# Mixture-of-experts half of a transformer block: experts written out without loops, routing two blocks ahead, expert weights spread by DMA and multiplied in on GpSimd

## What is computed

```python
x = x + attention(layernorm(x))        # 32 x 256 tokens, width 128, 16 heads, window of 128
h = layernorm(x)
scores = sigmoid(h @ gate_w.T)         # 16 experts in 4 groups
# the two best groups by (scores + bias), then the four best experts in them
w = picked scores / their sum * 2.5    # 12 of the 16 weights of a token are 0
g = einsum('th,eih->eti', h, gate_proj);  u = einsum('th,eih->eti', h, up_proj)
y = sum over experts of w[t,e] * ((silu(g) * u) @ down_proj[e].T)
x = x + y + (silu(h @ sh_gate.T) * (h @ sh_up.T)) @ sh_down.T
```

## Time and profile before

| | |
|---|---|
| runs | 808.34 us median of 3 (807.64 to 811.28) |
| the profiled execution's own time | 805.08 us |
| its span, first to last instruction | 803.3 us |
| mean granted TensorE clock | 0.966 of full speed |
| PE, DVE, ACT, POOL busy | 745.7, 599.4, 370.6, 174.2 us |
| attention half | 0 to about 400 us |
| expert half | about 403 to 803 us |

### The profile page before, as it was taken

The page is one execution under the profiler, slowest core; times in us unless marked ns, Lnnn a source line. Parts: engine busy times, 40 slices in busy tenths (PEclk is TensorE's granted clock), DMA queues, the critical chain, the costliest instruction groups (busy, mean ns, idle before and its releaser), DMA issues. The chain is left out here.

```text
span 803.3 us, 23092 instructions
## 1 busy us (share of the span) xinstructions
PE 745.7 (93%) x8627; PEld 483.5 (60%) x8627; DVE 599.4 (75%) x1870; ACT 370.6 (46%) x745; POOL 174.2 (22%) x285
## 2 busy tenths in 40 slices
PE   3598999999999999999699999999999999999997
PEld 2355666666666666665466566666656656666664
DVE  6777888787888888885477678776778767787764
ACT  2166677566666666674533322333223332233321
POOL 6522111122212222221022022120221202222000
PEclk9599999999999999996889999999999999999999
DMA  2136232322332333331011101111001111010000
GB/s 56 55 93 168 80 96 74 95 68 72 95 97 95 96 97 95 96 95 31 1 67 39 40 7 32 39 39 39 17 22 39 39 39 31 8 39 26 26 14 13
DMA packets 47410, 45.64 MB, mean 57 GB/s; under 512 B 10193, under 2 KB 38113, under 8 KB 47329
## 3 DMA queue, kind: packets, MB, share of 16 engines
q1 hardware_dynamic: 47328, 44.50, 18.1%
HBM read 27.44 MB, written 17.04 MB: 55 GB/s over the span
## 5 line engine op out<-in xcount | busy, mean ns | idle before, releaser
L913 DVE TENSOR_REDUCE chunkmax<-ps_max 128x16 f32<-128x512 f32 (+1 forms) x256 | 155.2, 647 | 37.6 <-PE ps_max L1303 37.6
L799 ACT ACTIVATE spare<-ps_max 128x512 f32<-128x512 f32 x144 | 86.0, 597 | 210.1 <-PE ps_max L1574 170.9
L715 ACT ACTIVATE probs<-ps_sc 128x512 f32<-128x512 f32 x256 | 139.0, 596 | 52.4 <-PE ps_sc L1340 51.3
L1590 PE MATMUL ps_c<-spare,wd 128*128 128x512 f32 x256 | 125.4, 592 | 0.0
L1129 DVE TENSOR_TENSOR spare<-spare,ps_sc 128x512 f32<-128x512 f32 x128 | 87.2, 681 | 20.5 <-ACT spare L799 11.7
L1137 DVE TENSOR_TENSOR spare<-spare,ps_att 128x512 f32<-128x512 f32 x128 | 87.2, 681 | 10.0 <-PE ps_att L1582 6.1
L1572 PE MATMUL ps_max<-xh,whigh 128*128 128x512 f32 x144 | 78.5, 545 | 0.0
L529 POOL TENSOR_TENSOR veps<-meanvar,eps 128x4 f32<-128x4 f32 x32 | 7.6, 238 | 317.1 <-DVE meanvar L877 317.1
L1364 PE MATMUL ps_sc<-qkstack 32*64 32x192 f16 (+2 forms) x2048 | 64.7, 234 | 11.0 <-issue 4.8
L1390 PE MATMUL ps_att<-probs,vdiag 128*32 128x192 f32 (+1 forms) x1536 | 71.4, 321 | 0.0
L1322 PE MATMUL ps_max<-hl,qdiag 32*128 32x160 f16 (+4 forms) x1024 | 50.7, 219 | 17.2 <-DVE chunkmax L913 10.3
(11 more groups left out here) (166 smaller groups left out, 1334.2 us busy)
## 6 DMA issues: line engine op xcount, KB each, us to landing
qkstack<-qk_scratch SPq DMA_DIRECT2D x48, 256.0 KB, 3.5
qk_scratch<-hl SPq DMA_DIRECT2D x32, 256.0 KB, 3.5
xin<-in_L_attn_x_dram SPq DMA_DIRECT2D x16, 256.0 KB, 3.2
x_scratch<-x SPq DMA_DIRECT2D x16, 256.0 KB, 2.2
xin<-x_scratch SPq DMA_DIRECT2D x16, 256.0 KB, 2.9
xres<-x_scratch SPq DMA_DIRECT2D x16, 256.0 KB, 2.7
out_dram<-result SPq DMA_DIRECT2D x16, 256.0 KB, 2.2
max_scratch<-rowmaxT SPq DMA_DIRECT2D x32, 8.0 KB, 1.4
```

Of the source, the lines that this page charges most:

```text
L715: nc.scalar.activation(dst[:, :], ps_sc[s][:, 0:dst.shape[1]], ACT.Exp, scale=SCALE).then_inc(probs_ready, 1)
L799: nc.scalar.activation(silu[slot][rows, :], ps_max[slot][rows, :], ACT.Silu).then_inc(silu_ready, 1)
L913: nc.vector.tensor_reduce(chunkmax[:, 2 * pair + m, at:at + CHUNKS[h]], ps_max[m][:, 0:BANK_COLS[h]].rearrange("p (n k) -> p n k", k=KB), ...
L1590: last = mm(ps_c[:, :], wd[:, p, :], inter[p % 3][:, :], start=(p == 0), stop=False)
```

## The change

The loops of the expert half are gone; every block is written out with plain integers. The rest, part by part:

- `spread_weight` and `pick` are gone, and so are the three bf16 parts of the weights. PE transposes the plain fp32 weights of block d + 1 (16 rows of 512) in unit 2 of block d, ACT copies them to `weightT`, SP stores these 32 KB to memory (`store_weight`) and loads them back with `partition_broadcast` (`load_spread`): two transfers of 64 partitions x 8 x 512 fp32, 2 MB together, into `spread[d % 2]`. That buffer lies over the attention half's `qkstack` and `vdiag`.
- `weigh` moves from DVE to POOL, in SBUF alone, with POOL's layer-norm steps between the units.
- The routing runs two blocks ahead; block 1 is routed in `last`, where the inputs of blocks 1 and 2 pass through the weight banks too. `xh` and `xl` have three buffers.
- `down` lags by three units throughout, across the block's edge as well. The small PE pieces are placed after given units.

```diff
-            def spread_weight(k, p):
-                if p == 0:
-                    pe.wait_ge(wpartsT_ready, k.count(1, 0))
-                pe.wait_ge(inter_ready, k.lag(NP + 1, p))
-                mm(ps_att[:, :], pick[:, p, :, :].rearrange("p a n -> p (a n)"), wpartsT[1 - k.parity][:, :],
-                   start=True, stop=True).then_inc(spread_done, 1)
...
-            def weigh(k, p):
-                dve.wait_ge(spread_done, k.lag(NP, p + 1))
-                dve.wait_ge(gated_ready, k.lag(NP, p + 1))
-                dve.wait_ge(down_done, k.lag(NP + 1, max(0, p - 2)))
-                tt(inter[p % 3][:, :], gated[(k.parity + p) % 2][:, :], ps_att[:, :], ALU.mult).then_inc(inter_ready, 1)
...
@@ GpSimd @@
+            def weigh(d, p):
+                if p == 0:
+                    pool.wait_ge(spread_loaded[d % 2], 32 * (d // 2 + 1))
+                pool.wait_ge(gated_ready, (NP + 1) * d + p + 1)
+                after(pool, down_done, (NP + 1) * d + p - 2)
+                nc.gpsimd.tensor_tensor(inter[p % 3], gated[p % 2], spread[d % 2][:, p, :], ALU.mult
+                                        ).then_inc(inter_ready, 1)
...
@@ VectorE @@
+            def gate(d, p):
+                n = (NP + 1) * d + p
+                dve.wait_ge(silu_ready, n + 1)
+                dve.wait_ge(u_done, NP * d + p + 1)
+                after(dve, inter_ready, NP * d + p - 1)
+                tt(gated[p % 2], silu[n % 2], ps_sc[n % 2][:, :], ALU.mult).then_inc(gated_ready, 1)
...
@@ SyncE @@
+            def store_weight(d):
+                if not valid(d):
+                    return
+                sp.wait_ge(weightT_ready, d + 1)
+                after(sp, spread_loaded[d % 2], 32 * (d // 2))
+                sp.dma_start(wt_d[d % 2], weightT[d % 2][:, :]).then_inc(weight_stored[d % 2], 16)
+            def load_spread(d):
+                if not valid(d):
+                    return
+                if d < 2:
+                    sp.wait_ge(pv_done, 6 * (STEPS - 1 + d))
+                else:
+                    sp.wait_ge(inter_ready, NP * (d - 1))
+                sp.wait_ge(weight_stored[d % 2], 16 * (d // 2 + 1))
+                src = wt_d[d % 2].rearrange("(n a) t -> a n t", a=2)
+                for a in range(2):
+                    sp.dma_start(spread[d % 2][I * a:I * a + I, :, :], src[a].partition_broadcast(I)
+                                 ).then_inc(spread_loaded[d % 2], 16)
...
@@ SyncE @@
+            for d in range(STEPS):
+                load_x1(d + 4)
+                load_residual(d)
+                store_weight(d + 1)
+                load_spread(d + 1)
+                if d > 0:
+                    store_result(d - 1)
...
@@ TensorE @@
+            def up(d, p):
+                n = (NP + 1) * d + p
+                after(pe, silu_ready, n - 1)
+                after(pe, gated_ready, n - 1)
...
-                down(k, NP - 2)
-                down(k, NP - 1)
-                down(k, NP)
...
@@ TensorE @@
+            for d in range(STEPS):
+                for p in range(NP + 1):
+                    up(d, p)
+                    n = (NP + 1) * d + p - 3
+                    if n >= 0:
+                        down(n // (NP + 1), n % (NP + 1))
+                    if p == 1:
+                        route(d + 2)
+                    if p == 2:
+                        transpose_weights(d + 1)
+                    if p == 4 and d > 0:
+                        transpose_y(d - 1)
+                    if p == 7:
+                        transpose_x1(d + 3)
```

More of the change, by code:

```diff
@@ L332, in high_of @@
                 return wrt[:, 0, :]
+            if what[0] == "x":
+                return xh[what[1]][:, :]
+            if what[0] == "weight":
+                return weightT[0][:, :]
             if what[0] == "down":
@@ new lines, in weigh @@
+            def weigh(d, p):
[5 more added lines that the diff above has]
+                                        ).then_inc(inter_ready, 1)
+            scale_weight(0)
+            scale_weight(1)
+            for d in range(STEPS):
+                more = d + 3 < STEPS
+                for p in range(NP):
+                    weigh(d, p)
+                    if p == 1 and more:
+                        inverse_deviation(STEPS + d + 3)
+                    if p == 2 and more:
+                        centre(STEPS + d + 3)
+                    if p == 3 and more:
+                        normalise(STEPS + d + 3)
+                scale_weight(d + 2)
@@ L1198, in _ @@
             last(STEPS - 1)
-            def ffn_first(k):
-                low_x(k.next())
-            def ffn_step(k):
-                more = not (k.j is None and k.c + 1 >= STEPS)
-                gate(k, 0)
-                weigh(k, 0)
-                sum_logits(k)
-                clip(k)
+            for d in range(STEPS):
+                route, more = d + 2 < STEPS, d + 3 < STEPS
+                if d > 0:
+                    low_x(d + 2)
+                gate(d, 0)
                 if more:
-                    tile_statistics(k.next(STEPS + 1), 0)
-                gate(k, 1)
-                weigh(k, 1)
-                invert(k)
+                    tile_statistics(STEPS + d + 3, 0)
+                gate(d, 1)
@@ new lines, in _ @@
+                if route:
+                    sum_groups(d + 2)
+                gate(d, 5)
+                if route:
+                    compare_groups(d + 2)
+                    count_wins(d + 2)
+                    mask_groups(d + 2)
+                gate(d, 6)
+                if route:
+                    find_best(d + 2)
+                    mark_best(d + 2)
+                gate(d, 7)
+                if route:
+                    choose_experts(d + 2)
+                    shares(d + 2)
@@ L1256, in _ @@
+                gate_shared(d)
+            add_y(STEPS - 1)
         @block.tensor
@@ new lines, in up @@
+            def up(d, p):
+                n = (NP + 1) * d + p
+                after(pe, silu_ready, n - 1)
+                after(pe, gated_ready, n - 1)
+                if p == 0 and d >= 3:
+                    pe.wait_ge(xl_ready, d - 1)
+                slot = n % 2
+                for q, bank in ((p, ps_max), (NP + p, ps_sc)) if p < NP else ((2 * NP, ps_max),):
+                    mm(bank[slot][:, :], whigh[:, q, :], xh[d % 3][:, :], start=True, stop=False)
+                    mm(bank[slot][:, :], whigh[:, q, :], xl[d % 3][:, :], start=False, stop=False)
+                    last = mm(bank[slot][:, :], wlow[:, q, :], xh[d % 3][:, :], start=False, stop=True)
```

605 lines of the change are left out of this document (262 added, 343 removed).

## The result

The changed kernel takes 761.55 us (median of 4 runs, 758.62 to 763.35), against 807.99 for the kernel before on the same chip (4 runs): a ratio of 0.942, 95% interval 0.939 to 0.945. The profiled execution took 758.62 us with a span of 756.8; that of before 805.1 with 803.3. The forecast was 765, with 753 to 788 as its range.

What follows compares the result with a forecast made beforehand. PE was taken to bound the expert half. Savings of 38 + 1 + 1.4 = 40.4 us from the profiled execution's 805.1 gave 764.7, put at 765 us, with a range of 753 to 788.

Steps and rivals of the forecast that it cites:

- PE bounds, and a spread costs 0.22 us: Expert half: PE sets the pace; removing eight spreads of 0.22 us takes 1.76 us of PE from each block.
- The blocks term: Expert half: 15 blocks at 22.2 us, 332 us in all against 370.2 before, so 38 us saved.
- the first block's: First expert block: 25 us instead of 26, partly at a lower clock, so 1 us saved.
- up to 1.9 us of a block are stalls: Expert blocks: products add up to 23.9 us, real blocks take 24.0 and 25.8; the stalls on `ps_att` go.
- The prediction's line on loops: Expert half: no branches and no reload of ACT's table; the effect is in the 25.8 us blocks, already counted.
- DVE at 12.9 us: Expert block: DVE loses eight products of 0.681 us, falling from 18.3 to 12.9 us of work in 22.2.
- rival B: Expert blocks: POOL holds up DVE's small steps, 5.4 us a block; 780 to 795 us in all. Chance 0.10.
- POOL: Expert block: `weigh` takes 1.285 us on POOL, 15.5 us at most in all; POOL bounds only above 2.1 each.
- DMA: Spread load per block: 10.4 us for 2.1 MB; cover 2.9 us to POOL, 7 to PE, beyond about one each.
- Rival C: Spread load late, over 18 us; at 22 us each block waits about 4, + 60, 825 us. Chance 0.05.
- The start: From attention projection to first expert product: experts begin at 402 instead of 403.45, bounds 399 and 406; 1.4 us saved.
- Tail: End of the kernel: stays at 4 us, nothing saved.

Runs made afterwards that it cites:

- the one-pass kernel: The changed kernel with its down products in the single-pass 32-bit format of the up products (lower precision of y): 735.20 us, ratio 0.907.

## Why the prediction was right, point by point

- **PE bounds, and a spread costs 0.22 us.** Right, twice: blocks of 22.03 us against the 22.2 taken (and 0.2 for small delays, which did not come), and 26.4 us back when eight such products were put in again. The blocks term was 38, and the first block's 1; measured together 40.1.
- **The stalls.** The step "up to 1.9 us of a block are stalls", with the waits on `ps_att` beside it, took the place where PE pays for the cause. The size was right, since it was read from the distance of the stores; but nearly all of it came with the loop's turns (10.3 us of the expert stretch). Of the 29.9 us of weight-load waits, 22.2 stay without loops and are all but free. The sum did not need the split, because the change removed both at once; that it came out with the cause misplaced is luck. The prediction's line on loops did say that their effect is in the 25.8 us blocks.
- **DVE at 12.9 us.** Mis-sized: 17.95, so 5.05 more. That is the mechanism of rival B, whose own figure was 5.4, held for DVE and, one stop apart, not for PE: 17.95 is under 22, and from 430 us on no block shows PE behind DVE. In the first block one does. There the first spread is late, and behind it steps in a row are shut out between the gates at 408.85 and 414.04, and PE stops 2.13 us (DVE's rows, then PE's):

```profile
409.64 1.20 DVE L1013 SCALAR_TENSOR_TENSOR score<-tanh_over,sigma_below 128x64 f32<-128x64 f32 x1
410.87 0.97 DVE L1017 SCALAR_TENSOR_TENSOR choice<-score,bias 128x64 f32<-128x64 f32 x1
411.88 2.25 DVE L1026 TENSOR_TENSOR pair_sums<-choice 128x48 f32<-128x48 f32 x3
```

```profile
414.87 0.47 PE L1560 MATMUL ps_max<-xh,whigh 128*128 128x512 f32 x1 [2.13 <-DVE probs L1105]
```

B's chance of 0.10 was for the time, not for the mechanism; the mechanism should have stood in the sum. The rule of "Who interferes with whom" in the Trainium skill's "SBUF — State Buffer" (two SBUF inputs, or a 2-port mode, which a copy can enter, contend with GpSimd; at most one SBUF input otherwise does not) fits: `chosen` with two operands in SBUF went from 0.225 to 1.27 us and the copy `needles` from 0.174 to 1.05, while `gate` with its one operand in SBUF stayed at 0.68 and `picked`, with one operand in PSUM, at about 0.22. That the copy runs in such a mode no run here shows.
- **POOL.** Right: 1.290 us against 1.285, 13.8 us a block against "15.5 at most". Doing the work twice showed that it adds up and then bounds; the threshold for a `weigh`, 2.1 us in the prediction, comes to 2.3 by the measured rows, an estimate.
- **DMA.** 10.4 us forecast, about 10.8 measured; it was there 3.5 us before GpSimd's first weighting (575.8 against 579.30), where the prediction had 2.9, and 8.8 before PE would have been held, where it had 7. What it had wrong is who is held first, which is DVE, at the third gate, and "beyond, each us costs about one": a chain 15 us longer cost 4 us in a block (26.0 against 22.03) and a stop of 13 in the first. Rival C had the same 4 us for about 12 more; that the two agree is partly luck. (That two such transfers serialize stands in the same page of the Trainium skill, under "Can I just issue two DMAs to hit both halves?", and not in the section that the prediction names; the rate near 200 GB/s while both loads are on their way agrees.)
- **The start.** Forecast 402, bounds 399 to 406; measured 397.08, outside. Twelve profiled executions bear on it. The last body's residual on GpSimd, up to which the changed kernel and the nine made from it are alike, began between 342.9 and 348.3 us in them; in the kernel before and its written-out form at 348.5 and 349.6. From there to the first expert product it took 52.2 to 54.7 us with the change and 55.0 and 55.3 without. In the two profiled executions that are compared, 2.5 of the 6.4 us lie behind that point and 3.9 ahead of it; over the twelve, the means differ by 1.2 behind it (53.9 against 55.1), near the 1.4 of the sum, and by 4.0 ahead of it (345.0 against 349.0). All ten with the change began earlier than both without, but the ten spread over 5.4 us. Whether the change moves the attention half stays open: no experiment separated it. So the term of the sum that was mis-sized is the start: 1.4 us where 6.4 were measured, with nothing in it for what lies ahead of the last residual.
- **Tail.** 4 us in both, as said.

The sum, 764.7 against the profiled execution's 758.6, was 6.1 us high: 1.1 for the expert stretch (39 forecast, 40.1 measured), 5 for the start.

## What to carry to other kernels

Undo a change in its parts before crediting any: here the products taken off PE and the written-out loops made 36.7 of the 40.1 us in the expert stretch, and handing work to GpSimd none of it, although it read as the main idea. Ask also what is late before blaming the place where an engine waits. A wait beneath a running instruction is not a cost until the distance between instructions says so: compare the block with the sum of its products. Before you count the cover of a late transfer, follow it to the first engine that waits for a buffer and has other work queued behind, not to the last consumer.

## What was not expected of the hardware

- A stop of PE of 3.20 us was followed by about 5 us at a granted clock of 0.50 (578.20 to 583.00), which costs some 2.4 us more than the stop itself; the block of the one-pass kernel shown above has stops of 1.0 and 1.6 us and was granted 1.00.
- A 256 KB transfer that is issued 4 us behind the 2 MB one lands after 8.9 us, where it took 2.2 to 2.9 before the change. That was free only because its consumer comes a block later.
- A loop's turn cost about 1.7 us every two blocks here, though the body was long; the trace of the kernel before shows a load of ACT's table in each turn, six of them in the stretch from 430 to 780 us, and the written-out kernel none. Two of PE's stops follow each load, 3.6 and 5.9 us behind the one at 604.45. That this load is what the turn costs was still not tested by itself.

The group in the trace of the kernel before:

```profile
L799 ACT ACT_TABLE_LOAD x6 | 7.7, 1283 | 4.1 <-PE ps_max L1574 4.1
```
